# Moving half of the residual addition from VectorE to ScalarE, by way of the accumulator banks

## The chip, the cores and the metric

The kernel runs on one core of a Trainium2 chip. The metric is the device time of one execution in microseconds (us), which is a little longer than the span of the profiled execution. The core's engines run unsynchronized, each through its own queue in order: TensorE (PE) multiplies, VectorE (DVE), ScalarE (ACT, which the words on the change call ActivationE) and GpSimd (POOL) work elementwise, and SyncE (SP) issues DMAs. They wait for each other on semaphores only.

## The reference

For 2048 tokens (64 sequences of 32) of width 512 the kernel computes `x + base + 2 * lora`:

```
base   = x @ W.T                                  # W 512 x 512
logits = x @ Wr.T + 5 * one_hot(language id)      # 8 experts
gates  = softmax over the two highest logits, 0 for the other six
h      = x @ A.T                                  # 8 experts x 16 ranks = 128 columns
lora   = (h * gates of its expert) @ B            # 128 x 512
out    = x + base + 2.0 * lora
```

Everything is fp32 in and out. The two highest logits decide which experts count, so the products must be nearly exact in fp32.

## The kernel before, in words

The tokens are 16 tiles of 128. fp32 operands are split into an upper part, rounded to fp32r, and a lower part, the remainder; a product is three matmuls (upper by upper, upper by lower, lower by upper), summed in PSUM.

Each tile t has two PSUM banks out of four pairs (t modulo SLOTS = 4). `heads_ps` takes 392 columns, called heads: the right half of the base product (256), h (128) and the logits (8). `base_ps` takes the left half of the base product (256 columns). To both halves the lora product is added later.

What TensorE does for tile t is step(t): heads(t), 12 matmuls of 392 columns; lora(t-3), four matmuls of 256 columns with the upper part `ghT_hi` of the gated h of tile t-3 and two with its lower part `ghT_lo`; base(t), 12 matmuls of 256 columns. Steps 3 to 13 are written like this; the tail interleaves tiles 13 to 15 by hand. heads(t) waits for the two parts of x of tile t and for `heads_read` of tile t-4, that is, until VectorE's `out_rest(t-4)` has read that bank; base(t) waits for `out_base(t-4)` in the same way. heads(4) is the first that has to wait for a bank.

VectorE does for each tile, in an order written out by hand: `best_two` (logits, MAX, index, cast, `den`), where `den` waits for the exponential `e` from ScalarE; `gates` (`second`, `rden`, `gate`); `gated` (`gh`, the gated h); `in_blocks` (`blocks`, transposed squares for the way through memory); later `ghT_lower` (`ghT_lo`), `out_rest` (`out_sb` from `heads_ps` and `x_sb`, right half) and `out_base` (the same from `base_ps`, left half).

ScalarE does `x_upper` (`x_hi`), `ghT_upper` (`ghT_hi`) and `exponential` (`e`). GpSimd does only `x_lower` (`x_lo`) in this stretch, right after each `x_hi`.

SyncE issues all DMAs of the main loop in order: for tile t it waits for `blocks(t)` and stores it to `gh_blocks`, then issues a load, if one is due (x transposed at even t; `x_sb` for tiles 6 to 8 at t = 3, 9 to 11 at t = 5, 12 to 15 at t = 7), waits until `blocks(t)` has been stored, loads it back as `ghT`, and stores the output of tile t-3. `ghT_upper(t)` waits for that load, for tiles 1 to 13; tiles 0, 14 and 15 are transposed on TensorE instead.

## Time and profile before

| what | us |
|---|---|
| median of 3 runs | 79.3 (79.08 to 79.88) |
| the profiled execution's own time | 79.36 |
| its span | 77.5 |
| TensorE busy | 72.9 (94%) |
| VectorE busy | 61.5 (79%) |
| GpSimd busy | 22.4 (29%) |
| ScalarE busy | 21.8 (28%) |

The busy times are sums over engines that overlap, so their shares do not say which one sets the end; the chain of waits does. Between the span and the profiled execution's own time lie 1.86 us in which no engine of the profile works. Matmuls overlap in their pipeline: the duration of one is longer than the distance from one start to the next.

### The profile page before, as it was taken

Reading aid. Unit: us, or ns where it says so; the run is one execution under the profiler, and the core shown is the slowest. Engines: PE = TensorE matmul, PEld = TensorE weight load, DVE = VectorE, ACT = ScalarE, POOL = GpSimd, SP = SyncE. Lnnn points to the kernel's source line nnn. Section 1 sums busy time; section 2 is a strip of 40 time slices with the busy share of each in tenths; the row PEclk is TensorE's granted clock in tenths of the full one; section 3 lists DMA queues with packets and bytes.
Section 4 is the critical chain, followed back from the end, with each engine's and each line's share of the span. In section 5 each row is a group of like instructions: output and inputs, shape, how many; then the busy total and the mean of one; then the engine's idle time right before and its main releaser. Section 6 shows DMA issues by size and latency. Waiting matters only on the chain.

```text
span 77.5 us, 1531 instructions
## 1 busy us (share of the span) xinstructions
PE 72.9 (94%) x489; PEld 69.5 (90%) x489; DVE 61.5 (79%) x233; ACT 21.8 (28%) x56; POOL 22.4 (29%) x26
## 2 busy tenths in 40 slices
PE   6999999999499999999999999999999999999960
PEld 2269999999399999999999999999999999999950
DVE  0097678888798989798988989796989889888860
ACT  1663943114505031130505040341405051103100
POOL 4054729003440606060412305042604115000000
PEclk9999999999999999999999999999999999999998
DMA  1999999301572898789579898270975515166073
GB/s 12 307 330 380 433 422 425 140 8 34 89 259 62 244 352 239 228 203 362 112 246 238 309 303 252 100 205 16 232 266 170 162 42 169 34 205 236 7 271 135
DMA packets 14214, 15.96 MB, mean 206 GB/s; under 512 B 7680, under 2 KB 10368, under 8 KB 14080
## 3 DMA queue, kind: packets, MB, share of 16 engines
q1 hardware_dynamic: 13920, 15.35, 62.0%
q10 hardware_dynamic: 288, 0.53, 2.0%
q8 instruction: 3, 0.05, 0.2%
q14 instruction: 3, 0.02, 0.1%
HBM read 10.84 MB, written 5.05 MB: 205 GB/s over the span
## 4 chain that ended last, share of the span: by engine, by line
PE 83%; DVE 11%; issue 2%; DVEq 0%
PE heads_ps L506 38%; PE base_ps L506 25%; PE heads_ps L538 5%; PE base_ps L538 5%; PE base_ps L576 4%; DVE top_atf L368 2%; PE heads_ps L542 2%; PE base_ps L542 2%; PE heads_ps L581 2%; DVE gh L388 1%; DVE top_at L366 1%; DVE second L375 1%; DVE blocks L351 1%; DVE top L363 1%; DVE gate L380 1%
## 5 line engine op out<-in xcount | busy, mean ns | idle before, releaser
L232 POOL TENSOR_TENSOR x_lo<-xT_sb,x_hi 128x512 fp32r<-128x512 f32 x14 | 18.1, 1292 | 37.2 <-ACT x_hi L271 35.8
L506 PE MATMUL heads_ps<-w_hi,x_hi 128*128 128x392 f32 x63 | 21.7, 352 | 1.1 <-DVE out_sb L401 1.1
L506 PE MATMUL heads_ps<-w_lo,x_hi 128*128 128x392 f32 x63 | 20.9, 340 | 0.0
L506 PE MATMUL heads_ps<-w_hi,x_lo 128*128 128x392 f32 x63 | 20.5, 339 | 0.0
L506 PE MATMUL base_ps<-w_hi,x_lo 128*128 128x256 f32 x64 | 17.6, 281 | 0.0
L506 PE MATMUL base_ps<-w_hi,x_hi 128*128 128x256 f32 x64 | 17.5, 283 | 0.0
L506 PE MATMUL base_ps<-w_lo,x_hi 128*128 128x256 f32 x64 | 17.4, 280 | 0.0
L287 ACT ACTIVATE e<-top 128x1 f32<-128x1 f32 x16 | 4.7, 296 | 37.6 <-DVE top L363 37.6
L506 PEld LDWEIGHTS heads_ps<-w_hi,x_hi 128*128 128x128 f32 x63 | 11.8, 190 | 1.6 <-ACT x_hi L271 1.3
L506 PEld LDWEIGHTS base_ps<-w_hi,x_hi 128*128 128x128 f32 x64 | 12.0, 189 | 0.4 <-issue 0.3
L506 PEld LDWEIGHTS base_ps<-w_lo,x_hi 128*128 128x128 f32 x64 | 12.1, 189 | 0.0
L506 PEld LDWEIGHTS base_ps<-w_hi,x_lo 128*128 128x128 f32 x64 | 11.9, 188 | 0.0
L506 PEld LDWEIGHTS heads_ps<-w_lo,x_hi 128*128 128x128 f32 x63 | 11.7, 188 | 0.0
L506 PEld LDWEIGHTS heads_ps<-w_hi,x_lo 128*128 128x128 f32 x63 | 11.7, 188 | 0.0
L375 DVE TENSOR_SCALAR second<-expert,top_atf,e 128x8 f32<-128x8 int32 x16 | 10.8, 678 | 0.0
L271 ACT ACTIVATE x_hi<-xT_sb 128x512 fp32r<-128x512 f32 x14 | 8.7, 619 | 1.9 <-DMA xT_sb<-in_xT 1.9
L401 DVE TENSOR_TENSOR out_sb<-heads_ps,x_sb 128x256 f32<-128x256 f32 x16 | 6.7, 416 | 0.5 <-PE heads_ps L542 0.4
L388 DVE SCALAR_TENSOR_TENSOR gh<-heads_ps,rden,gate 128x128 f32<-128x128 f32 x16 | 5.6, 351 | 1.7
L407 DVE TENSOR_TENSOR out_sb<-base_ps,x_sb 128x256 f32<-128x256 f32 x16 | 6.6, 411 | 0.0
L351 DVE STREAM_TRANSPOSE blocks<-gh 128x128 f32<-128x128 f32 x13 | 5.3, 406 | 0.4
L380 DVE SCALAR_TENSOR_TENSOR gate<-expert,top_atf,second 128x8 f32<-128x8 int32 x16 | 5.5, 343 | 0.0
L411 DVE TENSOR_TENSOR w_lo<-first_sb,w_hi 128x392 fp32r<-128x392 f32 (+1 forms) x8 | 4.5, 596 | 1.1 <-ACT w_hi L259 1.1
(46 smaller groups left out, 93.0 us busy)
## 6 DMA issues: line engine op xcount, KB each, us to landing
out<-out_sb SPq DMA_DIRECT2D x14, 256.0 KB, 2.9
x_sb<-in_x SPq DMA_DIRECT2D x4, 768.0 KB, 6.6
xT_sb<-in_xT SPq DMA_DIRECT2D x5, 512.0 KB, 4.5
x_sb<-in_x SPq DMA_DIRECT2D x1, 1024.0 KB, 7.5
first_sb<-in_first SPq DMA_DIRECT2D x2, 454.0 KB, 5.2
gh_blocks<-blocks SPq DMA_DIRECT2D x13, 64.0 KB, 2.1
ghT<-gh_blocks SPq DMA_DIRECT2D x13, 64.0 KB, 2.5
xT_sb<-in_xT SPq DMA_DIRECT2D x1, 768.0 KB, 7.4
```

Of the source, the lines that this page charges most:

```text
L232: nc.gpsimd.tensor_tensor(x_lo[:, s, :], xT_sb[:, t - len(FIRST), :], x_hi[:, s, :].bitcast(FP32), ALU.subtract).then_inc(x_lo_made, 1)
L271: nc.scalar.activation(x_hi[:, s, :], xT_sb[:, t - len(FIRST), :], ACT.Copy).then_inc(x_hi_made, 1)
L287: nc.scalar.activation(e2[:, :], top[:, 0:1], ACT.Exp, scale=-1.0, bias=top[:, 1:2]).then_inc(e2_made, 1)
L351: nc.vector.transpose(blocks[s][:, :].rearrange("p (j c) -> p j c", c=SQUARE), gh[s][:, :].rearrange("p (r j) -> p j r", r=SQUARE)).then_i ...
L375: nc.vector.tensor_scalar(second[:, :], expert[:, :], top_atf[:, 1:2], e2[:, :], ALU.is_equal, ALU.mult).then_inc(second_made, 1)
L380: nc.vector.scalar_tensor_tensor(gate[:, :], expert[:, :], top_atf[:, 0:1], second[:, :], ALU.is_equal, ALU.add).then_inc(gate_made, 1)
L388: nc.vector.scalar_tensor_tensor(gh[s][:, :].rearrange("p (e r) -> p e r", r=R), heads_ps[s][:, REST:REST + ER].rearrange("p (e r) -> p e ...
L401: nc.vector.tensor_tensor(out_sb[:, t, BASE:O], heads_ps[s][:, 0:REST], x_sb[:, t, BASE:O], ALU.add).then_inc(heads_read, 1)
L407: nc.vector.tensor_tensor(out_sb[:, t, 0:BASE], base_ps[s][:, 0:BASE], x_sb[:, t, 0:BASE], ALU.add).then_inc(out_made, 1)
L411: nc.vector.tensor_tensor(w_lo[:, k, cols], w_sb[:, k, cols], w_hi[:, k, cols].bitcast(FP32), ALU.subtract).then_inc(w_lo_made, 1)
L506: return nc.tensor.matmul(dst, xs[:, s, chunks[k]], ws[:, k, cols], start=(k == 0 and n == 0), stop=(k == KC - 1 and n == last_n))
L538: nc.tensor.matmul(dst, ghT_hi[s][:, :], bs[:, cols], start=False, stop=False, skip_group_check=True)
```

## The change

For tiles 4 to 14 VectorE's `out_base` (reading `base_ps` and `x_sb`, writing `out_sb`) is gone. Instead ScalarE copies the left half of x into `base_ps` before the tile's base product (`place_x`), TensorE sums the base product onto it (`base_onto_x`, with no start flag), and ScalarE copies the finished bank to `out_sb` (`copy_base`). Base(t) now waits for `place_x(t)`, which waits for the bank's last reader and for `x_sb` of tile t. The orders of ScalarE and VectorE are written anew, and stores wait for `copy_base`. TensorE has the same matmuls in the same order. (New names: `out_copied` counts copies, `x_placed` placements.) The core of the diff:

```diff
+PLACED = range(4, 15)
...
+            def base_out(t):
+                if t in PLACED:
+                    sp.wait_ge(out_copied, t - PLACED[0] + 1)
+                else:
+                    sp.wait_ge(out_made, t + 1 if t < PLACED[0] else t - len(PLACED) + 1)
 
...
                 if t >= LAG:
-                    sp.wait_ge(out_made, t - LAG + 1)
+                    sp.wait_ge(heads_read, t - LAG + 1)
+                    base_out(t - LAG)
                     store(t - LAG, 1)
...
+            def place_x(t):
+                s = t % SLOTS
+                if t < 2 * BATCH:
+                    act.wait_ge(x_first[t // BATCH], 16)
+                else:
+                    act.wait_ge(x_group, 16 * min(t // BATCH - 1, len(X_LOADS)))
+                if t - SLOTS < PLACED[0]:
+                    act.wait_ge(out_made, t - SLOTS + 1)
+                else:
+                    act.wait_ge(out_copied, t - SLOTS - PLACED[0] + 1)
+                nc.scalar.activation(base_ps[s][:, 0:BASE], x_sb[:, t, 0:BASE], ACT.Copy).then_inc(x_placed, 1)
+
+            def copy_base(t):
+                act.wait_ge(lora_base_done, t + 1)
+                nc.scalar.activation(out_sb[:, t, 0:BASE], base_ps[t % SLOTS][:, 0:BASE],
+                                     ACT.Copy).then_inc(out_copied, 1)
...
             exponential(2)
+            x_upper(4)
+            ghT_upper(1)
+            x_upper(5)
+            exponential(3)
+            place_x(4)
+            place_x(5)
+            ghT_upper(2)
+            exponential(4)
+            x_upper(6)
             t0, t1, t2 = range(TILES - 3, TILES)
-            for t in range(LAG, t0):
-                x_upper(t + 1)
-                if t > LAG:
-                    ghT_upper(t - LAG)
+            for t in range(5, t0):
+                if t - LAG in PLACED:
+                    copy_base(t - LAG)
+                place_x(t + 1)
                 exponential(t)
-            x_upper(t1)
-            ghT_upper(t0 - 3)
+                x_upper(t + 2)
+                ghT_upper(t - LAG + 1)
+            ghT_upper(t0 - 2)
+            copy_base(t0 - 3)
+            place_x(t1)
             exponential(t0)
-            ghT_upper(t0 - 2)
             x_upper(t2)
+            copy_base(t0 - 2)
             ghT_upper(t0 - 1)
             exponential(t1)
+            copy_base(t0 - 1)
             exponential(t2)
             ghT_upper(t0)
             ghT_upper(t1)
+            copy_base(t0)
             ghT_upper(t2)
+            copy_base(t1)
 
...
             gated(2)
+            out_rest(0)
             in_blocks(2, 2)
+            best_two(3)
+            out_base(0)
+            ghT_lower(1)
+            gates(3)
+            out_rest(1)
+            gated(3)
+            out_base(1)
+            in_blocks(3, 3)
+            best_two(4)
+            ghT_lower(2)
+            gates(4)
+            gated(4)
+            in_blocks(4, 0)
             t0, t1, t2 = range(TILES - 3, TILES)
-            for t in range(LAG, t0 - 1):
-                if t > LAG + 1:
+            for t in range(LAG + 2, t0 - 1):
+                if t > LAG + 2:
                     ghT_lower(t - LAG)
+                out_rest(t - LAG)
+                if t - LAG not in PLACED:
+                    out_base(t - LAG)
                 best_two(t)
-                out_rest(t - LAG)
-                out_base(t - LAG)
-                if t == LAG:
-                    ghT_lower(1)
                 gates(t)
                 gated(t)
                 in_blocks(t, t % SLOTS)
@@ -467,7 +523,6 @@
...
             in_blocks(t0 - 1, (t0 - 1) % SLOTS)
-            out_base(t0 - 4)
             ghT_lower(t0 - 3)
             best_two(t0)
             ghT_lower(t0 - 2)
@@ -475,25 +530,20 @@
             gates(t0)
             gated(t0)
             in_blocks(t0, t0 % SLOTS)
-            out_base(t0 - 3)
             out_rest(t0 - 2)
-            out_base(t0 - 2)
             ghT_lower(t0 - 1)
             best_two(t1)
             gates(t1)
             gated(t1)
             out_rest(t0 - 1)
-            out_base(t0 - 1)
...
+            def base_onto_x(s, ks):
+                for k in ks:
+                    for n in range(3):
+                        last = nc.tensor.matmul(base_ps[s][:, 0:BASE], (x_lo if n == 2 else x_hi)[:, s, chunks[k]],
+                                                (w_lo if n == 1 else w_hi)[:, k, base_cols], start=False,
+                                                stop=(k == KC - 1 and n == 2), skip_group_check=True)
                 return last
 
...
                 lora_of(t - LAG, (j - LAG) % SLOTS)
-                base_ready(t)
-                base(s, range(KC)).then_inc(base_done, 1)
+                if isinstance(t, int) and t < PLACED[0]:
+                    base(s, range(KC)).then_inc(base_done, 1)
+                else:
+                    pe.wait_ge(x_placed, t - PLACED[0] + 1)
+                    base_onto_x(s, range(KC)).then_inc(base_done, 1)
 
```

The first place is ScalarE's queue from the exponential of tile 2 on; `x_hi` is the next tile's upper part, `e` the exponential. Before:

```order
L287 ACTIVATE e<-top 128x1 [waits top_made]
L271 ACTIVATE x_hi<-xT_sb 128x512 [waits base_done,xT_group]
L287 ACTIVATE e<-top 128x1 [waits top_made]
L271 ACTIVATE x_hi<-xT_sb 128x512 [waits base_done,xT_group]
L277 ACTIVATE ghT_hi<-ghT 128x128 [waits ghT_landed1]
```

And with the change, up to tile 5's exponential and what follows it:

```order
L305 ACTIVATE ghT_hi<-ghT 128x128 [waits ghT_landed1]
L282 ACTIVATE x_hi<-xT_sb 128x512 [waits base_done,xT_group]
L315 ACTIVATE e<-top 128x1 [waits top_made]
L294 ACTIVATE base_ps<-x_sb 128x256 [waits out_made,x_first1] x2
L305 ACTIVATE ghT_hi<-ghT 128x128 [waits ghT_landed0]
L315 ACTIVATE e<-top 128x1 [waits top_made]
L282 ACTIVATE x_hi<-xT_sb 128x512 [waits base_done,xT_group]
L294 ACTIVATE base_ps<-x_sb 128x256 [waits out_made,x_group]
L315 ACTIVATE e<-top 128x1 [waits top_made]
L282 ACTIVATE x_hi<-xT_sb 128x512 [waits base_done,xT_group]
L305 ACTIVATE ghT_hi<-ghT 128x128 [waits ghT_landed1]
```

`ghT_hi` of tile 1 has moved ahead of `x_hi` of tile 5 and of tile 3's exponential. Tile 6's x is placed (the row that waits for `x_group`) ahead of tile 5's exponential, `x_hi` of tile 7 and `ghT_hi` of tile 3.

The second place is VectorE from `gh` of tile 2 to the first `ghT_lo` by way of memory, tile 1's. Before:

```order
L388 SCALAR_TENSOR_TENSOR gh<-heads_ps,rden,gate 128x128
L351 STREAM_TRANSPOSE blocks<-gh 128x128
L358 TENSOR_TENSOR logits<-heads_ps,bias 128x8
L363 MAX top<-logits 128x8
L366 MAX_INDEX top_at<-top,logits 128x8
L368 CAST top_atf<-top_at 128x2
L370 TENSOR_SCALAR den<-e 128x1
L401 TENSOR_TENSOR out_sb<-heads_ps,x_sb 128x256
L407 TENSOR_TENSOR out_sb<-base_ps,x_sb 128x256
L337 TENSOR_TENSOR ghT_lo<-ghT,ghT_hi 128x128
```

And with the change:

```order
L431 SCALAR_TENSOR_TENSOR gh<-heads_ps,rden,gate 128x128
L444 TENSOR_TENSOR out_sb<-heads_ps,x_sb 128x256
L394 STREAM_TRANSPOSE blocks<-gh 128x128
L401 TENSOR_TENSOR logits<-heads_ps,bias 128x8
L406 MAX top<-logits 128x8
L409 MAX_INDEX top_at<-top,logits 128x8
L411 CAST top_atf<-top_at 128x2
L413 TENSOR_SCALAR den<-e 128x1
L450 TENSOR_TENSOR out_sb<-base_ps,x_sb 128x256
L380 TENSOR_TENSOR ghT_lo<-ghT,ghT_hi 128x128
```

`out_rest(0)`, the addition from `heads_ps`, has moved from behind tile 3's `den` to right behind tile 2's `gh`.

The third place is ScalarE in tile 12, the last pass of its loop. With the change there stand, in this order:

```order
L298 ACTIVATE out_sb<-base_ps 128x256 [waits lora_base_done]
L294 ACTIVATE base_ps<-x_sb 128x256 [waits out_copied,x_group]
L315 ACTIVATE e<-top 128x1 [waits top_made]
L282 ACTIVATE x_hi<-xT_sb 128x512 [waits base_done,xT_group]
L305 ACTIVATE ghT_hi<-ghT 128x128 [waits ghT_landed0]
```

Tile 12's exponential has the copy of tile 9 and the placement of tile 13 ahead of it. On VectorE, tiles 6 to 11 have `out_rest(t-3)` ahead of `best_two(t)`, but for tile 12 it still stands behind it, as before.

## Rows read from the trace of the kernel before

**Rows 1.** The page: busy time by engine, and TensorE's clock in 40 slices.
```profile
PE 72.9 (94%) x489; PEld 69.5 (90%) x489; DVE 61.5 (79%) x233; ACT 21.8 (28%) x56; POOL 22.4 (29%) x26
...
PEclk9999999999999999999999999999999999999998
```

**Rows 2.** The chain that ended last: start us, us, what.
```profile
20.67 0.44 DVE out_sb L401
...
25.73 2.12 PE heads_ps L506 x12
...
28.33 0.12 PE heads_ps L542
...
29.98 2.12 PE heads_ps L506 x12
...
49.08 0.23 PE heads_ps L538
```

**Rows 3.** Timeline, TensorE: start us, us, what, idle before.
```profile
19.82 0.28 PE L506 MATMUL base_ps<-w_hi,x_lo 128*128 128x256 f32 x1
21.24 0.41 PE L506 MATMUL heads_ps<-w_hi,x_hi 128*128 128x392 f32 x1 [1.14 <-DVE out_sb L401]
```

**Rows 4.** Timeline, VectorE, tiles 2 and 3.
```profile
18.04 0.15 DVE L370 TENSOR_SCALAR den<-e 128x1 f32<-128x1 f32 x1
...
18.50 0.23 DVE L380 SCALAR_TENSOR_TENSOR gate<-expert,top_atf,second 128x8 f32<-128x8 int32 x1
18.83 0.35 DVE L388 SCALAR_TENSOR_TENSOR gh<-heads_ps,rden,gate 128x128 f32<-128x128 f32 x1
19.22 0.41 DVE L351 STREAM_TRANSPOSE blocks<-gh 128x128 f32<-128x128 f32 x1
...
21.34 1.06 DVE L337 TENSOR_TENSOR ghT_lo<-ghT,ghT_hi 128x128 fp32r<-128x128 f32 x1
...
23.36 0.41 DVE L351 STREAM_TRANSPOSE blocks<-gh 128x128 f32<-128x128 f32 x1
```

**Rows 5.** Timeline, ScalarE, the same stretch.
```profile
17.62 0.29 ACT L287 ACTIVATE e<-top 128x1 f32<-128x1 f32 x1 [1.50 <-DVE top L363]
17.83 0.62 ACT L271 ACTIVATE x_hi<-xT_sb 128x512 fp32r<-128x512 f32 x1
...
20.70 0.29 ACT L277 ACTIVATE ghT_hi<-ghT 128x128 fp32r<-128x128 f32 x1
```

**Rows 6.** Timeline, GpSimd: tiles 4 and 5, and tile 15.
```profile
18.64 1.29 POOL L232 TENSOR_TENSOR x_lo<-xT_sb,x_hi 128x512 fp32r<-128x512 f32 x1 [5.01 <-ACT x_hi L271]
20.98 1.28 POOL L232 TENSOR_TENSOR x_lo<-xT_sb,x_hi 128x512 fp32r<-128x512 f32 x1 [1.04 <-ACT x_hi L271]
...
63.60 1.32 POOL L232 TENSOR_TENSOR x_lo<-xT_sb,x_hi 128x512 fp32r<-128x512 f32 x1 [3.16 <-ACT x_hi L271]
```

**Rows 7.** Timeline, VectorE: tile 13's gate.
```profile
63.80 1.14 DVE L380 SCALAR_TENSOR_TENSOR gate<-expert,top_atf,second 128x8 f32<-128x8 int32 x1
```

**Rows 8.** The DMA that loads ghT of tile 1, issued at 18.65.
```profile
DMA to landing us min/median/max: 1.9/1.9/1.9
```

**Rows 9.** Timeline, SyncE's queue: the x_sb load for tiles 6 to 8.
```profile
24.16 0.44 SPq L168 DMA_DIRECT2D x_sb<-in_x  x1
```

**Rows 10.** That load, and the one for tiles 12 to 15.
```profile
DMA to landing us min/median/max: 4.5/4.5/4.5
...
DMA to landing us min/median/max: 7.5/7.5/7.5
```

**Rows 11.** Timeline, tile 15: the last lora product and its reader.
```profile
74.13 0.28 PE L542 MATMUL heads_ps<-b_hi,ghT_lo 128*128 128x256 f32 x1
...
74.45 0.42 DVE L401 TENSOR_TENSOR out_sb<-heads_ps,x_sb 128x256 f32<-128x256 f32 x1 [0.37 <-PE heads_ps L542]
```

**Rows 12.** Groups by line and form, ScalarE: SBUF to SBUF, PSUM to SBUF.
```profile
L259 ACT ACTIVATE w_hi<-first_sb 128x256 fp32r<-128x256 f32 x2 | 0.8, 418 | 0.5 <-DMA first_sb<-in_first 0.5
...
L283 ACT ACTIVATE ghT_hi<-base_ps 128x128 fp32r<-128x128 f32 x2 | 0.5, 265 | 2.3 <-PE base_ps L529 2.3
```

More of the change, by code:

```diff
@@ L153, in cond_resid_program @@
         out_made = sem("out_made")
+        x_placed = sem("x_placed")
+        out_copied = sem("out_copied")
         heads_cols, base_cols, all_cols = slice(0, HEADS), slice(HEADS, WIDTH), slice(0, WIDTH)
@@ L208, in _ @@
                 if t >= LAG:
-                    sp.wait_ge(out_made, t - LAG + 1)
+                    sp.wait_ge(heads_read, t - LAG + 1)
+                    base_out(t - LAG)
                     store(t - LAG, 1)
             for t in range(MOVED[-1] - LAG + 1, TILES - 2):
-                sp.wait_ge(out_made, t + 1)
+                sp.wait_ge(heads_read, t + 1)
+                base_out(t)
                 store(t, 1)
@@ L217, in _ @@
                 sp.dma_start(out[:, t, BASE:O], out_sb[:, t, BASE:O]).then_inc(out_stored, 16)
-                sp.wait_ge(out_made, t + 1)
+                base_out(t)
                 sp.dma_start(out[:, t, 0:BASE], out_sb[:, t, 0:BASE]).then_inc(out_stored, 16)
@@ L492, in _ @@
             out_rest(t0)
-            out_base(t0)
             out_rest(t1)
             ghT_lower(t2)
-            out_base(t1)
             out_rest(t2)
@@ L524, in base @@
                         last = base_product(s, k, n)
+                return last
+            def base_onto_x(s, ks):
[4 more added lines that the diff above has]
+                                                stop=(k == KC - 1 and n == 2), skip_group_check=True)
                 return last
@@ L557, in heads_ready @@
                     pe.wait_ge(heads_read, t - SLOTS + 1)
-            def base_ready(t):
-                if not (isinstance(t, int) and t < SLOTS):
-                    pe.wait_ge(out_made, t - SLOTS + 1)
             def step(t, j):
@@ L660, in _ @@
             heads(s2, range(KC)).then_inc(heads_done, 1)
-            pe.wait_ge(out_made, t2 - SLOTS + 1)
+            pe.wait_ge(out_copied, t2 - SLOTS - PLACED[0] + 1)
             transpose(t1)
-            base(s1, range(KC)).then_inc(base_done, 1)
+            pe.wait_ge(x_placed, t1 - PLACED[0] + 1)
+            base_onto_x(s1, range(KC)).then_inc(base_done, 1)
             lora_of(t0, s0)
@@ L667, in _ @@
             lora_of_tail(t1)
-            pe.wait_ge(out_made, t2 - SLOTS + 2)
+            pe.wait_ge(out_copied, t2 - SLOTS + 1 - PLACED[0] + 1)
             transpose(t2)
```

## The prediction, made before the changed kernel had run

> **What bounds the kernel now.** I read the page's busy times first, then the chain of waits, then the timelines around the only gap in TensorE's stream. TensorE is busy for 72.9 of 77.5 us, and its clock is granted in full (2.4 GHz) in all slices but the last [rows 1]. In the chain one step is 4.25 us (heads of tile 5 at 25.73, of tile 6 at 29.98), and from the start of a step, called S below, the last lora product into `heads_ps` starts at S + 2.60 (28.33) [rows 2]. From heads(4) on the chain is TensorE alone, step after step, with 0.1 us lost once where a `ghT_hi` came late (0.23 for a product that takes 0.12) [rows 2]. So only idle time of TensorE counts: a part that is late by more than its slack moves the end, and work taken from VectorE counts only where TensorE waits for it.
>
> There is one such place. The last product of base(3) starts at 19.82, heads(4) starts at 21.24, after 1.14 us of waiting for VectorE [rows 3]: `out_rest(0)` starts at 20.67, behind `best_two(3)` [rows 2].
>
> **What the change gives.** `out_rest(0)` now follows `gh(2)`, which starts at 18.83; the next operation there started 0.39 later [rows 4], so the addition runs from 19.22 to 19.64. Then heads(4) waits for `x_lo(4)` instead, which ends at 18.64 + 1.29 = 19.93 [rows 6] and is not moved; with 0.14 us to TensorE (21.24 against the addition's end at about 21.10) heads(4) starts at 20.07. **Term A: -1.17.** All later times are counted from this.
>
> The eleven additions that leave VectorE (0.41 us each, 4.5 in all) give nothing themselves: VectorE then waits longer for lora(t-3) or for heads(t). The 22 ScalarE operations are not shown in this trace. Bounds: 0.27 us, which a copy of half the columns out of PSUM took, and 0.62, which `x_hi` took for twice the columns [rows 5, 12]. Nearest is the copy of 128x256 within SBUF, 0.42 [rows 12]; the PSUM copy of 128x128 is a little shorter than its SBUF sister (0.27 against 0.29 [rows 5, 12]), so I take 0.42 for `place_x` and 0.38 for `copy_base`. ScalarE goes from 21.8 to about 31 us busy, with room. The Trainium skill ("VectorE: DVE Perf Modes", the errata section) gives ScalarE a smaller fixed cost from PSUM than from SBUF; I work out an estimate of 0.36 us for 256 columns from its table, by which the sum would be about 0.05 lower. No row here has this form.
>
> **What it takes back, first: ghT_lo(1).** ScalarE now does `ghT_hi(1)` before `x_hi(5)`. The load lands at 18.65 + 1.9 = 20.55 [rows 8], so `ghT_hi(1)` starts at 20.59 (20.70 before [rows 5]), `x_hi(5)` at 20.79, `e(3)` at 21.32. GpSimd's `x_lo(5)` follows the start of `x_hi` by 0.80 (17.83 to 18.64 [rows 5, 6]): 21.59 to 22.88. VectorE's `den(3)` waits for `e(3)`: 21.64; `out_base(0)` 21.77; `ghT_lo(1)` 22.09, in the middle of `x_lo(5)`. Before, the same operation started at 21.34 inside GpSimd's 20.98 to 22.26 and took 1.06 us, to 22.40, that is 0.14 after GpSimd's end [rows 4, 6]. So it ends at 23.02 and TensorE goes on at 23.16, where it wanted to at 20.07 + 2.60 = 22.67. **Term B: +0.5**; 0.14 if `ghT(1)` lands 0.35 sooner. The Trainium skill ("SBUF — State Buffer", SBUF: two separate sides) says that VectorE and GpSimd share one port pair as an exclusive lock, taken by whichever starts first; the trace agrees.
>
> **Second: tile 6's x, and lora(3).** From there VectorE does `second` 22.94, `out_rest(1)` 23.59, `gh(3)` 23.92, `out_base(1)` 24.31, and `blocks(3)` 24.64 to 25.05; before, `blocks(3)` ended at 23.77 [rows 4]. SyncE issues the `x_sb` load for tiles 6 to 8 0.39 after that (24.16 [rows 9]): now at 25.44, 1.3 us later. It took 4.5 us to land [rows 10], with the same kinds of transfer around it; I take 4.4: 29.85. Before, `x_sb(6)` was first needed by `out_rest(6)`, three steps later. Now `place_x(6)` waits for it in ScalarE's queue, and behind it stand `e(5)`, `x_hi(7)` and `ghT_hi(3)`. Its bank is free at about 29.15. So: `place_x(6)` 29.87, `e(5)` 30.20, `x_hi(7)` 30.40, `x_lo(7)` 31.20 to 32.49, `ghT_hi(3)` 30.93 to 31.22. `ghT_lo(3)` comes after `gh(5)` and `blocks(5)` at 32.02 and is held by `x_lo(7)` to 32.63. With S(6) = 29.06, lora(3) wants `ghT_hi` at 31.18 and gets it at 31.37, and wants `ghT_lo` at 31.85 and gets it at 32.78. **Term C: +1.1.** If x lands 1 us sooner, `out_base(2)` and the port are left: 0.45. If it takes the 7.5 us of the 1 MB load [rows 10], C is 4.2. It is nearest to its own row.
>
> **The steady steps** cost nothing more. lora(t-3) can be read by VectorE 0.32 after the start of its last product (74.13 to 74.45 [rows 11]). In step t ScalarE copies and places from about S + 3.05 on and starts `e(t)` at S + 3.85. `x_lo(t+2)` follows `e` by 1.02 (17.62 to 18.64), while `gate` follows `e` by 0.88 (to 18.50 [rows 4, 5, 6]) and is through. `x_lo` ends at S + 6.2, `ghT_lo` at S + 6.3, that is 2.05 into the next step, where it is wanted at 2.45. x is placed 3 us ahead of its use.
>
> **Third: tile 12.** There `out_rest(9)` stands behind `best_two(12)`, whose `den` waits for `e(12)`, and that now stands behind `copy_base(9)` and `place_x(13)`: `e(12)` at S + 3.85, `den` at 4.2, `out_rest(9)` 4.3 to 4.7, TensorE at 4.85 where it wanted 4.25: 0.57. The same at tile 13: 0.05. **Term D: +0.6**; 0.4 with 0.3 us per ScalarE operation, 1.0 with 0.6. In the tail the last operations follow TensorE as before: 0. The 0.1 us at lora(7) goes, since `ghT(7)`'s store is earlier in its step: **-0.1**.
>
> **Sum:** -1.17 + 0.49 + 1.12 + 0.62 - 0.09 = +0.97, on the profiled execution's 79.36: 80.33. That execution is 0.06 above the median, so 80.3. The forecast's own range is 79.7 to 81.6: its lower end with C at its low value, its upper end with C 1 us larger (x landing in 5.4 us) and D at 1.0.
>
> **Rivals.**
> 1. *Half is given back.* x lands early enough that only the bank and the port hold `place_x(6)`, and the ScalarE operations are short: -1.17 + 0.14 + 0.45 + 0.4 - 0.1 = -0.3, 79.0 after the 0.06; with one of the three at its full size up to 80.0. For it: each return is a few tenths over a slack of tenths. Chance 0.31.
> 2. *The gain stays, faster.* `ghT_lo(1)` and `ghT_lo(3)` find the port free, and `out_rest(9)` is in time: 79.36 - 1.17 = 78.2. For it: the queues have room. Against it: the row of 1.06 us, and D rests on order alone. Chance 0.10, 78.0 to 78.5. That the additions don't come sooner at all would be the mirror of it, no A, but returns: about 81.5; `out_rest(0)` depends only on lora(0), so I give it nothing.
> 3. *The port takes the gate in every step.* At tile 13 `gate` started at 63.80, after `x_lo` at 63.60, and took 1.14 us instead of 0.23 [rows 4, 6, 7]. The margin in the new order is 0.14 to 0.2 us. If it is lost, `gate` ends 0.03 after `x_lo`, at e + 2.34; then gh 0.10, blocks 0.39, `ghT_lo` 0.33 and its 0.27, TensorE 0.15, the lora product readable 0.42, copy and placement 0.84 to the next e: 4.84 us per step against 4.25. From tile 6 to 12 that is 7 x 0.59 = 4.1 on top: 84.4. The lock of the skill's SBUF page would do this if GpSimd came first. It decides from an `x_hi` 0.2 us earlier against `gate`. For `gate` being through: it was at tile 2, in the very order that the loop now has. Chance 0.06.
>
> The forecast keeps 0.53. Its cases and rival 1 reach from 79.0 to 81.6; outside lie rivals 2 and 3 and about 0.04 at the edges: **80.3, range 79.0 to 81.6**. What a measurement of this kernel tells from no change is about 1%, 0.8 us: under 78.5 lies rival 2, 0.10; 78.5 to 80.1 rival 1 with the forecast's low end, 0.31 + 0.05; above it 0.54.
>
> **What would show it.** A: heads(4) starts near 20.1, after `x_lo(4)`. B: the first `ghT_lo` by way of memory takes about 0.9 us, and TensorE idles for it at 22.7. C: ScalarE idles before a `base_ps<-x_sb` near 29 to 30 us until a DMA lands, and TensorE has its largest gap at 31 to 33. D: about 0.6 us of TensorE's idle time before heads(13), released by VectorE's `out_sb`. Steps of 4.25 us between 34 and 60. It is wrong if `x_sb` is there before its bank is free, if `gate` is the long operation in most steps, or if a placement takes more than 0.5 us.

## The result, and the profile after

| | median, us | ratio to before | 95% interval |
|---|---|---|---|
| before | 79.42 | | |
| changed | 81.25 (81.06 to 81.69) | 1.022 | 1.018 to 1.026 |

The change makes the kernel 2.2% slower, 1.8 us. Forecast were 80.3 us, a range of 79.0 to 81.6, and slower as the likeliest. The profiled execution took 81.69 us, the slowest of the four, with a span of 79.9. Here and below, medians are over all executions of a kernel, while ratios and their intervals leave out those more than 1.5% above its fastest.

The page after, busy time by engine and TensorE's clock (answers [rows 1]):

```profile
PE 74.7 (94%) x489; PEld 70.0 (88%) x489; DVE 55.0 (69%) x222; ACT 29.1 (36%) x78; POOL 22.3 (28%) x26
...
PEclk9999999999999999999999999999999999999999
```

VectorE is busy 6.5 us less, ScalarE 7.3 more, the clock is full, and the end is later. The 6.5 us are not the additions alone. By the durations of the operations, which overlap a little, the eleven additions are 4.5 us less, one small operation, `second`, is 5.1 less, and `ghT_lo` is 1.5 more. `second` in the groups by line and form, before and after:

```profile
L375 DVE TENSOR_SCALAR second<-expert,top_atf,e 128x8 f32<-128x8 int32 x16 | 10.8, 678 | 0.0
...
L418 DVE TENSOR_SCALAR second<-expert,top_atf,e 128x8 f32<-128x8 int32 x16 | 5.7, 356 | 0.0
```

Alone `second` takes 0.28 us. In the kernel before it took 1.16 to 1.27 in seven of its sixteen calls (tiles 4 to 9 and 11), each beside an `x_lo` of GpSimd, and the steps there still took 4.24 to 4.33 us. A row of it:

```profile
29.50 1.17 DVE L375 TENSOR_SCALAR second<-expert,top_atf,e 128x8 f32<-128x8 int32 x1
```

What counts is the distance from the start of heads(t) to that of heads(t+1), read from TensorE's timeline; heads(3) starts at 15.57 before and at 15.84 after.

| from heads to heads | before | after | difference | what holds TensorE after |
|---|---|---|---|---|
| 3 to 4 | 5.67 | 4.40 | -1.27 | |
| 4 to 5 | 4.33 | 4.81 | +0.48 | `ghT_lo(1)` |
| 6 to 7 | 4.25 | 5.41 | +1.16 | `ghT_lo(3)` |
| 8 to 9 | 4.24 | 4.59 | +0.35 | `ghT_hi(5)` |
| 10 to 11 | 4.33 | 4.34 | 0 | `ghT_hi(7)`, in both |
| 12 to 13 | 4.25 | 4.79 | +0.54 | `out_rest(9)` |
| 13 to 14 | 4.95 | 5.08 | +0.13 | the same, less |
| 14 to 15 | 2.84 | 3.20 | +0.36 | `ghT_lo(12)` |
| all others | | | 0 | |

The differences add up to 1.75, 1.77 with the hundredths of the others; the medians differ by 1.83. The two profiled executions differ by more, 2.4 us of span: besides the 1.77, heads(3) starts 0.27 later, and the last stores end 0.35 later after VectorE's last operation (2.5 us instead of 2.15). What those two are worth in the median one pair of profiles cannot tell.

**heads(4) and lora(1).** The timeline after, all engines: start us, us, engine, line, what, idle before. It answers [rows 3 to 6].

```profile
19.30 0.41 DVE L444 TENSOR_TENSOR out_sb<-heads_ps,x_sb 128x256 f32<-128x256 f32 x1
...
20.24 0.42 PE L556 MATMUL heads_ps<-w_hi,x_hi 128*128 128x392 f32 x1
...
21.80 1.29 POOL L243 TENSOR_TENSOR x_lo<-xT_sb,x_hi 128x512 fp32r<-128x512 f32 x1 [1.66 <-ACT x_hi L282]
...
22.24 0.99 DVE L380 TENSOR_TENSOR ghT_lo<-ghT,ghT_hi 128x128 fp32r<-128x128 f32 x1
...
23.29 0.39 PE L600 MATMUL heads_ps<-b_hi,ghT_lo 128*128 128x256 f32 x1 [0.20 <-DVE ghT_lo L380]
```

heads(4) has no releaser any more: the gap of 1.14 is gone. `ghT_lo(1)` starts inside `x_lo(5)`, ends 0.14 after it, and TensorE waits.

**lora(3).** The same view, later:

```profile
26.40 1.29 POOL L243 TENSOR_TENSOR x_lo<-xT_sb,x_hi 128x512 fp32r<-128x512 f32 x1 [3.31 <-ACT x_hi L282]
26.41 1.30 DVE L423 SCALAR_TENSOR_TENSOR gate<-expert,top_atf,second 128x8 f32<-128x8 int32 x1
...
28.83 0.41 DVE L450 TENSOR_TENSOR out_sb<-base_ps,x_sb 128x256 f32<-128x256 f32 x1
...
30.18 0.39 ACT L294 ACTIVATE base_ps<-x_sb 128x256 f32<-128x256 f32 x1 [3.94 <-DMA x_sb<-in_x]
...
30.50 0.28 ACT L315 ACTIVATE e<-top 128x1 f32<-128x1 f32 x1
...
31.47 1.27 POOL L243 TENSOR_TENSOR x_lo<-xT_sb,x_hi 128x512 fp32r<-128x512 f32 x1 [3.78 <-ACT x_hi L282]
32.25 0.65 DVE L380 TENSOR_TENSOR ghT_lo<-ghT,ghT_hi 128x128 fp32r<-128x128 f32 x1
...
32.95 0.38 PE L600 MATMUL heads_ps<-b_hi,ghT_lo 128*128 128x256 f32 x1 [0.68 <-DVE ghT_lo L380]
```

`place_x(6)` idles ScalarE for 3.94 us until x has landed, though its bank was free at 29.24. Tile 5's exponential follows only then, and the whole chain of tile 5 behind it. The first two rows show something that the prediction did not have: tile 4's `gate` took 1.30 us instead of 0.23. The late load covered it here; experiments 3, 7, 8 and 10 show what it costs where the load does not.

**heads(13), and lora(12).** The same view, twice:

```profile
59.41 0.38 ACT L298 ACTIVATE out_sb<-base_ps 128x256 f32<-128x256 f32 x1 [2.45 <-PE base_ps L600]
59.89 0.39 ACT L294 ACTIVATE base_ps<-x_sb 128x256 f32<-128x256 f32 x1
60.21 0.28 ACT L315 ACTIVATE e<-top 128x1 f32<-128x1 f32 x1
60.52 0.15 DVE L413 TENSOR_SCALAR den<-e 128x1 f32<-128x1 f32 x1 [0.84 <-ACT e L315]
60.60 0.42 DVE L444 TENSOR_TENSOR out_sb<-heads_ps,x_sb 128x256 f32<-128x256 f32 x1
...
61.17 0.42 PE L556 MATMUL heads_ps<-w_hi,x_hi 128*128 128x392 f32 x1 [0.39 <-DVE out_sb L444]
...
66.01 1.37 DVE L418 TENSOR_SCALAR second<-expert,top_atf,e 128x8 f32<-128x8 int32 x1
66.07 1.29 POOL L243 TENSOR_TENSOR x_lo<-xT_sb,x_hi 128x512 fp32r<-128x512 f32 x1 [3.60 <-ACT x_hi L282]
...
68.77 0.28 DVE L380 TENSOR_TENSOR ghT_lo<-ghT,ghT_hi 128x128 fp32r<-128x128 f32 x1
...
69.11 0.38 PE L600 MATMUL heads_ps<-b_hi,ghT_lo 128*128 128x256 f32 x1
```

The first six rows are a line of engines without a gap: copy, placement, exponential, `den`, `out_rest(9)`, TensorE. In the lower rows tile 13's `second` lasts 1.37 us, because `ghT_lo(11)` and `out_rest(10)` stand between `den` and it and `x_lo(15)` holds it up, although the row has `second` starting 0.06 us before `x_lo`; `ghT_lo(12)` at the end of that chain is late.

### The profile page after: what moved, and what is told of

It reads as the page before. It is cut to its first block, busy times and chain, and to the rows that moved or that the text cites. A ratio compares the mean times of both kernels' runs of the same rounds, so it can differ in the third digit from the quotient of the medians.

```text
span 79.9 us, 1567 instructions
## 1 busy us (share of the span) xinstructions
PE 74.7 (94%) x489; PEld 70.0 (88%) x489; DVE 55.0 (69%) x222; ACT 29.1 (36%) x78; POOL 22.3 (28%) x26
## 4 chain that ended last, share of the span: by engine, by line
PE 57%; DMA 21%; DVE 12%; issue 3%; ACT 3%; SPq 0%; DVEq 0%; ACTq 0%
PE heads_ps L556 24%; PE base_ps L580 11%; DMA ghT<-gh_blocks 10%; DMA x_sb<-in_x 6%; DMA gh_blocks<-blocks 6%; PE base_ps L556 5%; PE base_ps L633 4%; PE heads_ps L596 4%; PE base_ps L596 3%; PE heads_ps L600 2%; PE heads_ps L638 2%; DVE gh L431 2%; DVE top_atf L411 2%; PE base_ps L600 2%; DVE blocks L394 1%
## 5 line engine op out<-in xcount | busy, mean ns | idle before, releaser
L580 PE MATMUL base_ps<-w_hi,x_hi 128*128 128x256 f32 x44 | 12.4, 282 | 0.0
L580 PE MATMUL base_ps<-w_hi,x_lo 128*128 128x256 f32 x44 | 12.4, 281 | 0.0
L580 PE MATMUL base_ps<-w_lo,x_hi 128*128 128x256 f32 x44 | 12.3, 280 | 0.0
L298 ACT ACTIVATE out_sb<-base_ps 128x256 f32<-128x256 f32 x11 | 4.2, 383 | 14.8 <-PE base_ps L600 14.8
L580 PEld LDWEIGHTS base_ps<-w_lo,x_hi 128*128 128x128 f32 x44 | 8.3, 189 | 0.0
L580 PEld LDWEIGHTS base_ps<-w_hi,x_hi 128*128 128x128 f32 x44 | 8.3, 188 | 0.0
L580 PEld LDWEIGHTS base_ps<-w_hi,x_lo 128*128 128x128 f32 x44 | 8.2, 187 | 0.0
L294 ACT ACTIVATE base_ps<-x_sb 128x256 f32<-128x256 f32 x11 | 4.3, 389 | 9.9 <-DVE out_sb L450 5.4
L380 DVE TENSOR_TENSOR ghT_lo<-ghT,ghT_hi 128x128 fp32r<-128x128 f32 x13 | 6.2, 474 | 1.5 <-ACT ghT_hi L305 1.5
L305 ACT ACTIVATE ghT_hi<-ghT 128x128 fp32r<-128x128 f32 x13 | 3.9, 301 | 6.1 <-DMA ghT<-gh_blocks 5.9
```

The costliest lines, as they stand in the source:

```text
L294: nc.scalar.activation(base_ps[s][:, 0:BASE], x_sb[:, t, 0:BASE], ACT.Copy).then_inc(x_placed, 1)
L298: nc.scalar.activation(out_sb[:, t, 0:BASE], base_ps[t % SLOTS][:, 0:BASE], ACT.Copy).then_inc(out_copied, 1)
L380: nc.vector.tensor_tensor(ghT_lo[s][:, :], ghT[s][:, :], ghT_hi[s][:, :].bitcast(FP32), ALU.subtract).then_inc(ghT_lo_made, 1)
L580: last = nc.tensor.matmul(base_ps[s][:, 0:BASE], (x_lo if n == 2 else x_hi)[:, s, chunks[k]], (w_lo if n == 1 else w_hi)[:, k, base_cols], ...
```

## The experiments

Each was compared with the kernel before on the same chip, where that took 79.5 to 79.7 us in the median. Steps are distances between starts of heads, as in the table above. In the expectations the letters A to D are the prediction's terms.

**1. The earlier addition alone** (the kernel before with it).

```diff
             gated(2)
+            out_rest(0)
             in_blocks(2, 2)
...
-                out_rest(t - LAG)
+                if t > LAG:
+                    out_rest(t - LAG)
```

> The kernel before with one edit: out_rest(0) stands right behind gh(2), as in the change; all other additions stay on VectorE and no x is placed. My theory (each stall of TensorE comes from an order): heads(4) starts near 20.1 instead of 21.2, but out_rest(1) is still behind den(4) and out_base, so heads(5) waits about 1.1 us for it and lora(1) about 0.3: the wait moves one tile on, 79.4 to 79.9, no gain. Rival (the placing on ScalarE is what costs, the earlier addition is a plain gain): 78.2 to 78.4.

Measured: 79.74 us, ratio 1.002 (0.998 to 1.005). Steps: 3 to 4 took 4.38, but 4 to 5 took 5.19, and TensorE's timeline shows the wait there:

```profile
25.14 0.45 PE L508 MATMUL heads_ps<-w_hi,x_hi 128*128 128x392 f32 x1 [0.68 <-DVE out_sb L401]
```

The wait had moved on by one tile. What I had not expected is 10 to 11 at 4.95, 0.62 us more than before, where `ghT_hi(7)` waited for its DMA until 48.99.

**2. The same with VectorE's whole new order for tiles 2 to 4, and no placing.**

```diff
             gated(2)
+            out_rest(0)
             in_blocks(2, 2)
+            best_two(3)
+            out_base(0)
+            ghT_lower(1)
+            gates(3)
+            out_rest(1)
+            gated(3)
+            out_base(1)
+            in_blocks(3, 3)
+            best_two(4)
+            ghT_lower(2)
+            gates(4)
+            gated(4)
+            in_blocks(4, 0)
...
-            for t in range(LAG, t0 - 1):
+            for t in range(LAG + 2, t0 - 1):
```

> The kernel before with VectorE's order of the change for tiles 2 to 4 (out_rest(0) behind gh(2), out_rest(1) inside tile 3's gates, and so on), every addition still on VectorE, ScalarE's order untouched, no placing. My theory: the wait for the heads bank moves on, from heads(4) by lora(1) (0.3) and lora(2) (0.6) to heads(6) (about 1.1), since from tile 5 on out_rest(t-3) stands behind best_two(t) again: 79.8 to 80.5, a little slower than before. Rival (the earlier additions are a plain gain that the placing eats): 78.2 to 78.6.

Measured: 80.05 us, 1.006 (1.003 to 1.009). Step 5 to 6 took 5.52, with 0.77 us of idle time before heads(6) released by `out_sb`; step 10 to 11 took 4.74. The wait had moved on by two tiles.

**3. x of tiles 6 to 8 loaded at the start** (the change with it).

```diff
             load(x_sb, x, BATCH, BATCH, x_first[1])
+            load(x_sb, x, X_LOADS[LAG][0], X_LOADS[LAG][1], x_group)
...
-                elif t in X_LOADS:
+                elif t in X_LOADS and t > LAG:
```

> The change, with x_sb of tiles 6 to 8 loaded right behind the first six tiles at the start, instead of at t = 3. My theory: place_x(6) no longer waits for a DMA but for out_base(2), and goes about 1 us sooner; term C falls from 1.16 to about 0.45, and the wait for ghT(5) (0.34 in the change, a transfer that started late because step 6 was late and had the x_sb load for tiles 9 to 11 beside it) goes too: 1.0 us less than the change, 80.2 to 80.5. Rival (the waits come from ScalarE being loaded or from the port, whatever x does): no difference beyond 0.2. Rival (crowded transfers): the same bytes at another time make another ghT late, no gain or a loss.

Measured: 80.81 us, 1.010 (1.007 to 1.014), 0.3 above what I expected. Step 6 to 7 took 4.62 instead of 5.41 (an extra of 0.37; 0.45 was forecast), 8 to 9 took 4.24 instead of 4.59. ScalarE's timeline shows who releases the placement now:

```profile
30.10 0.39 ACT L295 ACTIVATE base_ps<-x_sb 128x256 f32<-128x256 f32 x1 [3.12 <-DVE out_sb L451]
```

That `out_sb` is `out_base(2)`, and it is late because `gate(4)` ahead of it was held again:

```profile
27.16 1.32 DVE L424 SCALAR_TENSOR_TENSOR gate<-expert,top_atf,second 128x8 f32<-128x8 int32 x1
```

Heads(3) started at 16.69 in this execution, later than in any other (15.54 to 16.35), so the earlier load may have cost something at the start; one profile cannot tell.

**4. The exponential of tile 3 first** (the change with it).

```diff
             x_upper(4)
+            exponential(3)
             ghT_upper(1)
             x_upper(5)
-            exponential(3)
```

> The change, with ScalarE's e(3) ahead of ghT_hi(1) and x_hi(5). My theory: den(3) comes 0.6 us sooner, ghT_lo(1) starts before GpSimd's x_lo(5) and takes 0.28 instead of 0.99 us; TensorE's 0.48 at lora(1) goes, blocks(3) and the x_sb load go 0.7 us sooner, so place_x(6) too: 0.5 to 0.9 us less than the change, 80.4 to 80.8. If the port lock is not the cause, ghT_lo(1) still takes about 1 us wherever it stands, and nothing is gained.

Measured: 81.45 us, 1.018 (1.011 to 1.025), which cannot be told from the change; I had expected 80.4 to 80.8. The profiled execution took 80.37, and in its timeline the mechanism is as expected:

```profile
21.34 0.28 DVE L380 TENSOR_TENSOR ghT_lo<-ghT,ghT_hi 128x128 fp32r<-128x128 f32 x1
...
21.71 1.29 POOL L243 TENSOR_TENSOR x_lo<-xT_sb,x_hi 128x512 fp32r<-128x512 f32 x1 [1.84 <-ACT x_hi L282]
```

0.28 us instead of 0.99, and step 4 to 5 took 4.27 instead of 4.81. The step is shown, a gain in the median is not: its other five executions took 80.61 to 82.78.

**5. The order at tiles 12 and 13** (the change with it).

```diff
             ghT_lower(t0 - 4)
-            best_two(t0 - 1)
             out_rest(t0 - 4)
+            best_two(t0 - 1)
...
             ghT_lower(t0 - 3)
-            best_two(t0)
             ghT_lower(t0 - 2)
             out_rest(t0 - 3)
+            best_two(t0)
```

> The change, with out_rest(9) ahead of best_two(12) on VectorE, and out_rest(10) and ghT_lo(11) ahead of best_two(13). My theory: out_rest no longer waits for an exponential that stands behind a copy and a placement; the 0.54 before heads(13) goes, and gates(13) follows den at once, so x_lo(15) does not hold `second` and the 0.36 before heads(15) goes: 0.6 to 0.9 us less than the change, 80.4 to 80.7. Rival (ScalarE's added work costs in itself): no gain, another wait in the tail takes its place.

Measured: 80.36 us, 1.008 (1.004 to 1.012). Steps 12 to 13, 13 to 14 and 14 to 15 took 4.25, 4.94 and 2.85, as before, where the change had 4.79, 5.08 and 3.20. All 1.03 us came back. But step 10 to 11 took 5.43 in its profile, in code that it shares with the change up to there:

```profile
49.93 0.38 PE L596 MATMUL heads_ps<-b_hi,ghT_hi 128*128 128x256 f32 x1 [0.92 <-ACT ghT_hi L305]
```

**6. The port takes a gate operation in every step** (the change with ScalarE's `x_hi(t+2)` ahead of `e(t)`).

```diff
                 place_x(t + 1)
-                exponential(t)
                 x_upper(t + 2)
+                exponential(t)
```

> The change, with x_hi(t+2) ahead of e(t) in ScalarE's loop (t = 5 to 12) and nothing else. GpSimd's x_lo then starts 0.2 to 0.5 us before VectorE's gate instead of 0.2 after it. By my third rival's mechanism gate or second takes 1.1 to 1.3 us in every step instead of 0.23, the steps become 4.8 us instead of 4.25 from tile 6 to 12, and the time is 4 to 5 us above the change: 85 to 87. If VectorE and GpSimd do not exclude each other, gate keeps its 0.23 us and the time stays within 1 us of the change (den comes 0.5 us later, inside the slack).

Measured: 87.1 us, 1.091 (1.084 to 1.097). One step in its timeline:

```profile
46.64 1.30 POOL L243 TENSOR_TENSOR x_lo<-xT_sb,x_hi 128x512 fp32r<-128x512 f32 x1 [3.53 <-ACT x_hi L282]
46.75 1.21 DVE L418 TENSOR_SCALAR second<-expert,top_atf,e 128x8 f32<-128x8 int32 x1
...
48.00 0.23 DVE L423 SCALAR_TENSOR_TENSOR gate<-expert,top_atf,second 128x8 f32<-128x8 int32 x1
...
49.05 0.25 DVE L380 TENSOR_TENSOR ghT_lo<-ghT,ghT_hi 128x128 fp32r<-128x128 f32 x1
...
49.35 0.39 PE L600 MATMUL heads_ps<-b_hi,ghT_lo 128*128 128x256 f32 x1 [0.32 <-DVE ghT_lo L380]
```

Two adjacent instructions changed places, and the steps from 8 to 12 take 4.84, 4.84, 4.92 and 4.85 us. It is `second` that is caught, not `gate`. But these four steps are only 2.0 of the 5.6 us between heads(3) and heads(15) by which this kernel is slower than the change. Another 1.1 is step 12 to 13 (5.91: `out_rest(9)` waits behind a still later exponential), and 2.5 are steps 6 to 7 and 7 to 8, which took 7.49 and 4.63 (5.41 and 4.25 in the change). There TensorE idled for 1.69 us in front of a product of lora(3), and then its granted clock fell, as the page shows:

```profile
33.89 0.38 PE L600 MATMUL heads_ps<-b_hi,ghT_lo 128*128 128x256 f32 x1 [1.69 <-DVE ghT_lo L380]
...
PEclk9999999999999999579999999999999999999999
```

From 34.2 to 36.8 us it was 0.50 (the level of 1.2 GHz), and base(6)'s twelve products took 2.56 us instead of 1.41; it was full again by 38.5. With the first heads(7) products that is about 1.5 us, an estimate from the distances between starts. So the time fell near my 85 to 87 in part for a reason that I had not thought of.

**7. Three orders mended together**: 4 and 5, and `place_x(6)` behind `ghT_hi(3)`, where base(6) still gets it in time.

```diff
-                place_x(t + 1)
+                if t > 5:
+                    place_x(t + 1)
                 exponential(t)
                 x_upper(t + 2)
                 ghT_upper(t - LAG + 1)
+                if t == 5:
+                    place_x(t + 1)
```

> The change with orders alone mended and no DMA moved: e(3) ahead of ghT_hi(1) and x_hi(5) (as in b2), place_x(6) behind e(5), x_hi(7) and ghT_hi(3) instead of ahead of them, and the tail order of b3. Same operations, same placing. My theory: terms B, C and D all go and A stays; steps of 4.25 us throughout, and against before only the 1.2 us of heads(4) is gained: 78.2 us. If ghT(7) is late as in a1 and b3 (0.6 and 1.1 us of waiting at lora(7), a transfer with the 1 MB load of x_sb ahead of it), that is taken off the gain: 78.2 to 79.3. Rival (placing and copying on ScalarE cost in themselves): stays above 79.8, with longer steps.

Measured: 79.87 us, 1.000 (0.996 to 1.004), above what I expected and where the rival had it, but not with the rival's longer steps: in its profile (79.31) the steps from 3 to 13 are 4.23 to 4.37 but 6 to 7, 4.58. There `gate(4)` took 1.31 us beside `x_lo(6)`.

**8. And the load split in two** (the counts that `place_x` and VectorE's additions wait for follow it, in 9 to 11 too).

```diff
-X_LOADS = {3: (6, 3), 5: (9, 3), 7: (12, 4)}
+X_LOADS = {3: (6, 3), 5: (9, 3), 7: (12, 2), 9: (14, 2)}
```

> c1 with the x_sb load for tiles 12 to 15 (1 MB, issued at t = 7) split in two: 12 and 13 at t = 7, 14 and 15 at t = 9. If the wait of lora(7) comes from ghT(7) queued behind the 1 MB load, it shrinks from up to 1.1 us to under 0.3, and the time is 78.0 to 78.5, up to 0.8 less than c1. If the wait comes from elsewhere (the block's own store, or chance), c1 and c2 are the same within 0.3.

Measured: 78.56 us, 0.990 (0.985 to 0.994). `ghT(7)` landed 3.1 us after its issue instead of 5.1. Step 6 to 7 is still 4.59, and the timeline shows why:

```profile
25.51 1.29 POOL L247 TENSOR_TENSOR x_lo<-xT_sb,x_hi 128x512 fp32r<-128x512 f32 x1 [2.79 <-ACT x_hi L286]
25.52 1.30 DVE L430 SCALAR_TENSOR_TENSOR gate<-expert,top_atf,second 128x8 f32<-128x8 int32 x1
```

`gate(4)` is held, as in 3, 7 and the change. Between it and `den(4)` stands `ghT_lo(2)`, 0.28 us. Starting 0.01 us sooner would not have been enough: over all traces here, the calls of `second` that started 0.07 us or less before `x_lo` were held as well, those that started 0.11 or more before it were not.

**9. The split alone, in the kernel before.**

```diff
-X_LOADS = {3: (6, 3), 5: (9, 3), 7: (12, 4)}
+X_LOADS = {3: (6, 3), 5: (9, 3), 7: (12, 2), 9: (14, 2)}
```

> The kernel before with the x_sb load for tiles 12 to 15 split as in c2 (12 and 13 at t = 7, 14 and 15 at t = 9), and nothing else. In before's profiled execution TensorE loses 0.1 us at lora(7), since its step there is late enough to cover ghT(7). My theory: 79.0 to 79.5, at most 0.4 less than before; the gain of c2 over c1 (1 %) appears only where the earlier steps are faster. Rival (the split is a plain gain of 1 % to which the change adds nothing): 78.5.

Measured: 79.31 us, 0.997 (0.994 to 1.001): no gain by itself. Step 10 to 11 took 4.25.

**10. And x_hi(6) kept back until gate(4) is made** (8 with one wait more).

```diff
             exponential(4)
+            act.wait_ge(gate_made, 5)
             x_upper(6)
```

> c2 with one wait more: ScalarE's x_hi(6) waits until VectorE's gate(4) is made. In c2 x_lo(6) starts 0.01 us before gate(4), which takes 1.30 us for it, and TensorE still loses 0.34 us at lora(3) in step 6. My theory: gate(4) takes 0.23, gh(4), blocks(4), e(5) and ghT_lo(3) come 0.5 to 1 us sooner, step 6 takes 4.25 to 4.30 instead of 4.59, and the time is 0.3 us less than c2, 78.2. If ghT_lo(3) is late for another reason, step 6 stays at 4.6.

Measured: 78.42 us, 0.985 (0.980 to 0.990), the fastest of all, 1.3 us under before on its chip. Its timeline has the two operations in the other order:

```profile
26.04 0.23 DVE L431 SCALAR_TENSOR_TENSOR gate<-expert,top_atf,second 128x8 f32<-128x8 int32 x1
...
27.11 1.29 POOL L247 TENSOR_TENSOR x_lo<-xT_sb,x_hi 128x512 fp32r<-128x512 f32 x1 [4.07 <-ACT x_hi L286]
```

Every step from heads(4) to heads(13) is 4.24 or 4.25, so nothing holds TensorE there. From heads(3) to heads(14) it takes 47.54 us, where before took 49.00; 0.50 of this 1.46 is lost at the start, where heads(3) comes at 16.07 instead of 15.57. Against 8 the medians differ by 0.14 us, within the intervals; step 6 to 7 shows the 0.34.

**11. No placing, but the order and the split** (2 with the split of 9, and both additions ahead of `best_two(t)`).

```diff
-                best_two(t)
                 out_rest(t - LAG)
                 out_base(t - LAG)
+                best_two(t)
                 gates(t)
```

> a2 (every addition on VectorE) with the split load and, from tile 5 on, both additions of tile t-3 ahead of best_two(t), the order that the change has. It asks whether the placing is needed at all. My theory: VectorE has 0.33 us a step too much for this order in the first tiles; TensorE waits 0.2 at lora(1), 0.6 at lora(2) and 0.5 at lora(3): 79.2 to 79.9, no gain over before, while c2 with the same idea gains 1 %. Rival (placing gives nothing, orders and the split do it all): 78.3 to 78.7, as c2.

Measured: 80.48 us, 1.009 (1.005 to 1.013), above what I expected. Steps 5 to 6, 6 to 7 and 11 to 12 took 4.59, 4.80 and 5.04. These orders without the placing gain nothing. But `x_lo` is in two of the three losses:

```profile
25.78 1.37 DVE L341 TENSOR_TENSOR ghT_lo<-ghT,ghT_hi 128x128 fp32r<-128x128 f32 x1 [0.49 <-ACT ghT_hi L281]
...
51.78 1.14 DVE L384 SCALAR_TENSOR_TENSOR gate<-expert,top_atf,second 128x8 f32<-128x8 int32 x1
```

`ghT_lo(2)` and `gate(10)` are held here, and ScalarE's order, the tail's order and the wait of 10 were not carried over. So this run does not say what the best order without the placing would take; that was not run.

**12. Number 10 with the 1 MB load whole.**

```diff
-X_LOADS = {3: (6, 3), 5: (9, 3), 7: (12, 2), 9: (14, 2)}
+X_LOADS = {3: (6, 3), 5: (9, 3), 7: (12, 4)}
```

> e2 with the x_sb load for tiles 12 to 15 whole again (1 MB at t = 7). c1 and c2 differ by 1 % in their medians, but the profiled execution of c1 shows no wait at lora(7). My theory: with every earlier step at 4.25 us ghT(7) lands later than TensorE wants it in most executions: a wait of 0.2 to 1.2 us before lora(7), 0.3 to 1.3 us more than e2 in the median, 78.7 to 79.7. If the split does not matter and c1's median was chance, this is e2's time, 78.4 within 0.3.

Measured: 78.48 us, 0.987 (0.984 to 0.991), the same as 10. My expectation fell. `ghT_hi(7)` was later, but not late:

```profile
47.29 0.31 ACT L305 ACTIVATE ghT_hi<-ghT 128x128 fp32r<-128x128 f32 x1 [1.04 <-DMA ghT<-gh_blocks]
```

So I can't put the 1% between 7 and 8 down to the split. In their profiled executions (79.31 and 78.19) the steps are alike, and 0.81 of the 1.12 us is there before the change's code begins: heads(3) starts at 16.35 in 7 and at 15.54 in 8. Why 7's start was later, and why three of its twelve executions took over 80 us (up to 81.48), stays open.

## Why the prediction was right, point by point

**What bounds the kernel** was right: the 1.77 us between heads(3) and heads(15) are idle time of TensorE, and the 4.25 us of a step did not change.

**Term A** was -1.17 and measured -1.27. It is a gain only together with what follows: alone it moves the wait to heads(5) (experiment 1), and VectorE's new order without the placing moves it to heads(6) (2).

**The eleven additions "give nothing themselves".** As a sentence on the change this held: VectorE's 4.5 us less of additions bought nothing there. As a sentence on what the additions are worth it may be too narrow: the best kernel with the placing stands at 0.985 (10), those without it at 0.997 to 1.009 (9, 1, 2, 11). Since 10 and 11 differ in more than the placing, and 11's losses pass through operations held by `x_lo`, how much of this is the placing's is not shown. Sizes: `place_x` took 0.39 (I took 0.42), `copy_base` 0.38, as taken; in the groups by line and form these are

```profile
L298 ACT ACTIVATE out_sb<-base_ps 128x256 f32<-128x256 f32 x11 | 4.2, 383 | 14.8 <-PE base_ps L600 14.8
...
L294 ACT ACTIVATE base_ps<-x_sb 128x256 f32<-128x256 f32 x11 | 4.3, 389 | 9.9 <-DVE out_sb L450 5.4
```

which answers [rows 12]. The estimate of 0.36 us that I had worked out from the Trainium skill's table ("VectorE: DVE Perf Modes", the errata section) for a source in PSUM was 0.02 short; either gives the same sum within 0.1.

**Term B** was +0.5 and measured +0.48; 4 takes the operation out of the port's way, and the term is gone from the steps. In 4, 6 and 10 an operation of 0.23 to 0.28 us takes that, or up to 1.3, by whether it or `x_lo` starts first. That is the exclusive lock, held for the whole instruction, of which the Trainium skill speaks ("SBUF — State Buffer", SBUF: two separate sides), as far as VectorE is the one that waits. "First" is blurred by some hundredths in the trace (8), and that GpSimd waits for VectorE no row here shows: `x_lo` never took more than 1.33 us, whatever ran when it started.

**Term C** was +1.1 and measured +1.16, of which 3 took out 0.79 by moving the load (I had 0.67). x landed 4.7 us after its issue (I took 4.4). What is left without the wait for the load, 0.33 to 0.37 in 3, 7 and 8, I had put at 0.45 and on `out_base(2)` and on `ghT_lo(3)` beside `x_lo(7)`. It was `gate(4)`, held by `x_lo(6)`, which made `out_base(2)` and tile 5's chain late: 8 and 10 differ in one wait that frees `gate(4)`; in 10 `ghT_lo(3)` is still held (0.51 us), and step 6 to 7 takes 4.25. So the size was about right and that part of the mechanism was not.

**Term D** was 0.57 and 0.05, and measured 0.54 and 0.13. 5 took both out.

**Where it fell short.** The sum was +0.97 and came out at +1.77. Two sentences failed. "In the tail the last operations follow TensorE as before: 0": it left out that tile 13's `second` has two operations between `den` and itself, and that `x_lo(15)` would overtake it, +0.36; 5 shows it. I had checked the port for each step of the loop and for `ghT_lo`, but not for the hand-written tail. And "The 0.1 us at lora(7) goes": it did not, and beside it came +0.35 at lora(5). The load of `ghT(5)` landed after 5.7 us where it had taken 4.6 before. `blocks(5)` is not what was late: its store was issued 2.36 us before the start of heads(7), before it was 2.21. But the store landed after 2.9 us instead of 1.9, so that the load was issued later, and the load was slower too. In both kernels the `x_sb` load for tiles 9 to 11 is issued between the two; it landed after 6.6 us instead of 4.3. In 3, where C is smaller, the 0.35 is gone; in 5, where C is as it was (step 6 to 7: 5.14), it is gone too and 1.18 us appear at lora(7) instead. So this part varies from execution to execution of the same code, and I can say only that ghT's way through memory has no slack left here in some of them. A term for it, a few tenths, belonged in the sum and not only in the range. The range held 81.25 by 0.35 us, with an upper end that I had built from x landing 1 us later and dearer ScalarE operations; x landed 0.3 later and the operations were as cheap as taken, so that the time lies inside it is in part luck. Two bounds were also added up wrong: by its own terms the forecast's lower end is 79.6, not 79.7, and rival 1 with term C at its full size is 79.7, not 80.0. Neither moves the range.

**The rivals.** Half given back: no. Faster: no. The port in each step: not in each, but the change had it at tiles 4 and 12 (`gate` 1.30 and 1.23 us) and at tile 13. I had named only tiles 2 and 13 of before; its trace has `second` held in seven tiles and `gate` in two (12 and 13), with steps of 4.24 to 4.33 us up to heads(13), so a held operation costs nothing where the chain has room. 6 shows the cost where it has none, 4.84 us a step. That this is my figure to the hundredth is chance: I had left out the 0.27 us of `gate`, which follows the held `second`, and had counted 0.2 us from `e` to `x_hi`, which 6 does not have.

## What to carry to other kernels

When TensorE's stream has one gap, moving the late operation forward can just move the gap to the next tile, as it did here (1, 2); and work taken away bought nothing until the order used the room (the change against 10). An operation that waits for a load or for TensorE should stand in its queue behind everything that others are waiting for: one placement ahead of one exponential cost 0.8 us here. And for each pair of engines that exclude each other, ask at every place, the tail too, which starts first and by how much, and whether the one that is held has room: about 0.1 us of head start decided 1.1 us of one operation, and that cost TensorE nothing in most tiles of the kernel before and 0.34 us in one step of 8.

## What the runs showed of the hardware that I had not expected

- Beside GpSimd's `x_lo`, these operations of VectorE took longer: `second` and `gate` (8 columns, 0.23 to 0.29 us alone, up to 1.39 held), `ghT_lo` (0.25 to 0.29 alone, up to 1.38 held) and the cast of the index (2 columns, 0.17 alone, 1.32 at 12.33 in the kernel before, with `x_lo` in its first tiles). They ended 0.01 to 0.04 us after `x_lo`, `ghT_lo` about 0.15 after it. Not every operation with its inputs in SBUF is held: the transpose took its 0.41 us (19.22 beside `x_lo` from 18.64 to 19.93, before), and MAX, the index, `den` and `rden` took their usual time too. So did the additions that take one input from PSUM (before, `out_base` at 21.01 took 0.41 us beside `x_lo` from 20.98 to 22.26).
- An operation can be held that starts a little ahead of `x_lo` in the trace: `second` was held from 0.07 us ahead (1.39 us, in 7) and 0.06 ahead (1.37, the change), and was not from 0.11 ahead (0.28, in 2).
- TensorE's granted clock fell to 0.50 after it had idled 1.69 us (6), for 2.6 us at least; after 0.68 us of idle time at the same place in the change, and after 1.14 us before heads(4) in the kernel before, it stayed full.
- A copy of 128x256 by ScalarE took 0.418 us from SBUF to SBUF, 0.389 from SBUF to PSUM and 0.383 from PSUM to SBUF.
- TensorE's products took as long summed onto x that ScalarE had written as with a start of their own: 1.41 us for twelve, in both kernels.
